# Fourteen row tiles a layer instead of seven, gathered by SyncE, with the adjacency counts and degree sums moved forward

## The chip, the cores and the metric

The kernel runs on one core of a Trainium2 chip. The metric is the device time of one execution in microseconds (us), as the median of several runs. The profile is one more execution, recorded by the hardware; its span runs from the first instruction to the last. Engines are named TensorE (PE), VectorE (DVE), ScalarE (ACT), GpSimd (POOL) and SyncE (SP).

## The reference

A graph of 2500 nodes with 256 features and 82,500 edges, sorted by destination. Two stages, each with a residual and a layer norm:

```python
# stage 1: two layers of RelGraphConv (8 relations)
for l in range(2):
    W = einsum('rb,bio->rio', coeff[l], basis[l])
    msg = einsum('ni,rio->rno', h, W)[etype, src] * norm
    h = segment_sum(msg, dst) + bias[l]          # relu after the first
x = layernorm(x + h)
# stage 2: three layers of mean aggregation
h = x @ W_in + b_in
for l in range(3):
    agg = segment_sum(h[src], dst) / max(deg, 1)
    h = relu(agg @ W_agg[l] + h @ W_self[l] + b_hid[l])
out = layernorm(x + h @ W_out + b_out)
```

## The kernel before

The edges are cut into T = 645 tiles of 128. In stage 1 each tile's 128 source rows of 256 floats are brought into SBUF and multiplied by a selection matrix that VectorE makes from destination, edge type and weight. TensorE does this for three tiles at a time (`pe_sums_of`, L1037); it adds weight times source row into (destination, relation) columns. Every 30 tiles form a window of 128 destinations, which is multiplied by the relation matrices (`pe_apply`, L885), gets its bias and is stored: in layer 0 as rows of H1 in DRAM, the table that layer 1 gathers from, in layer 1 as X1.

**Who fetches the rows.** GpSimd issues one indirect DMA for each tile (`rows_of`, L352) into 16 slots; a slot is free again when the tile that used it is summed (semaphore `s_sum`). Seven tiles of a layer, `ROW_TILES` (96, 180, ..., 600), are left out of GpSimd's list (`POOLED`). SyncE brings those as 128 plain DMAs of one row each (`sp_rows`, L1136), into one of two row buffers in the spare columns of `ei`. It reads the row addresses from SBUF into registers, eight at a time (L1133, one TENSOR_LOAD). The order is written out: `row_plan` spreads a row tile's 128 rows over the steps from the last row tile less 12 to its own less 12 (`ROW_LEAD`), and step t of SyncE's list holds what TensorE's step t stands beside.

**What else stands in SyncE's list,** in program order with the rows: in layer 0 the store of each finished window to H1 (`sp_store`, L1095, its base row loaded at L421), for which it waits on ScalarE's L784; in layer 1 the store of X1 and a load of x for two windows later (`sp_post`, L1095 and L1103), for which it waits on VectorE's L602; a load of 128 rows of the adjacency (`sp_load_rows`, L1173) for each window; and 20 loads for the degree sums (`sp_load_degrees`, L1182).

**Work beside the sums.** The dense adjacency for stage 2 is counted on TensorE from one-hot matrices (`pe_counts`, L867 and L868), ScalarE casts the counts and stores them. `adjacency_plan` says beside which tile: one count tile every 1.5 tiles from tile 90 on, and what is left up to 375 between the layers. In layer 1 from step 92 on the first mean aggregation is done in pieces (`pe_unit`), the degree sums at steps 426 to 545 (`D_BLOCK`, `pe_degree`, L1002; its data is loaded by SyncE at steps 418 + 6q), the degrees' columns at 548, the products of the nodes' own features at `OWN_TILES` (L950). Behind layer 1 follow the rest of the mean layers with TensorE busy throughout.

Of the kernel before, what the change touches and what calls it, by code (L numbers as in the profile page):

```python
# [15 lines left out]
N = 2500  # L16
D = 256
# [16 lines left out]
NG = 16  # L34
ROW_TILES = [96 + 84 * j for j in range(7)]
ROW_LEAD = 12
ROW_PARTS = range((len(ROW_TILES) + 3) // 4)
NSL = 8
# [37 lines left out]
def adjacency_plan():  # L76

    plan, a = {}, 0
    for n in range(2 * T):
        while a < T and n >= 90 + a * 1.5:  # L80
            plan.setdefault(n, []).append(a)
            a += 1
        if n == T - 1:
            while a < 375:
                plan.setdefault("between", []).append(a)
                a += 1
    assert a == T
    return plan
# [6 lines left out]

def row_plan():

    plan = {}
    for j, tile in enumerate(ROW_TILES):
        lo, hi = (ROW_TILES[j - 1] - ROW_LEAD if j else 2), tile - ROW_LEAD  # L100
        for r in range(128):
            plan.setdefault(lo + r * (hi - lo) // 128, []).append((j, r))
    return plan
# [5 lines left out]
LASTG = len(GROUPS) - 1  # L109
ROWS = row_plan()  # L110

POOLED = [n for n in range(2 * T) if n % T not in ROW_TILES]
PLACE = {n: p for p, n in enumerate(POOLED)}
# [55 lines left out]
def program(nc, x, ramp, ramp_col, src_rows, srcT, dstT, etT, wT, large, small, basis, coeff, bias, W_in, b_in, W_agg, W_self,  # L169
# [11 lines left out]
    with ExitStack() as ctx:  # L181
# [106 lines left out]
        s_land = [sem(f"s_land{i}") for i in range(NG)]  # L288
        s_ix, s_at, s_row = sem("s_ix"), sem("s_at"), [sem("s_row0"), sem("s_row1")]
        s_sel, s_sum = sem("s_sel"), sem("s_sum")  # L290
# [255 lines left out]
        def dve_unit(e, gi, c, mo):  # L546

            q, o = unit_of(gi, c, mo), sagg[:, mo, c * CH:(c + 1) * CH]
            e.wait_ge(s_part, q + 1)
            if gi == 0:  # L550
                e.tensor_copy(o, unit_bank(q)[:, 0:CH]).then_inc(s_acc, 1)
            else:
                e.wait_ge(s_acc, q - 2 * NC + 1)
                if gi > 7 and c < 3:
                    e.wait_ge(s_owns, 2 * c + mo + 1)
                e.tensor_tensor(o, unit_bank(q)[:, 0:CH], o, ALU.add).then_inc(s_acc, 1)  # L556
# [86 lines left out]
        def dve_layer(e, l):  # L643
            for t in range(T + (TAIL if l == 0 else 2)):
                n = l * T + t
                for u in range((0 if l == 0 else AHEAD) if t == 0 else t + AHEAD - 1, min(T, t + AHEAD)):
                    dve_select(e, l * T + u)
                if l == 0 and t == 20:
                    e.wait_ge(s_ix, 16 * len(ROW_PARTS))
                    at = di[0:32 * len(ROW_PARTS) - 31, 0:512]  # L650
                    e.tensor_scalar(at, at, 4 * D, None, ALU.mult).then_inc(s_at, 1)
                if l == 0 and t == 600:
# [21 lines left out]
                if l == 1:  # L674
                    for gi, c, mo in UNITS.get(t - 1, []):
                        dve_unit(e, gi, c, mo)
                    if t == 420:
# [3 lines left out]
                    if t == 549:  # L681
# [136 lines left out]
        def act_layer(e, l):  # L818
            for t in range(T + (TAIL if l == 0 else 2)):
                n = l * T + t  # L820
                if l == 0 and t == T + 10:
                    act_fix(e, 0)
                if l == 1 and t == 0:
                    act_fix(e, 1)
                if l == 1 and t % TA == TA - 1 and t < FIX - 2 * TA:
                    act_fix(e, t // TA + 2)
                if t == 0:
                    if l == 0:
                        e.wait_ge(s_zero, 1)
                    for k in range(4):  # L830
                        act_clear(e, l, 0, k)
                if t % TW in (24, 25, 26, 27) and t // TW + 1 < NW and t < T:
                    act_clear(e, l, t // TW + 1, t % TW - 24)
                for g, k in STEPS[l].get(t, []):
                    act_post(e, l, g, k)
                if l == 0 and LAG <= t < 8 * WPE + LAG:
                    act_weight(e, t - LAG)
                if t < T:
                    for a in COUNTS.get(n, []):
                        act_counts(e, a)  # L840
                if l == 1:
# [161 lines left out]

        def row_number(l, t):

            return l * len(ROW_TILES) + ROW_TILES.index(t)

        def pe_sums_of(e, l, t):
# [13 lines left out]
            for c in range(2):  # L1022
# [3 lines left out]
                for i in range(TA):  # L1026
                    n, k = l * T + t - TA + 1 + i, edge_rows(t - TA + 1 + i)
                    if n in PLACE:
                        rows = G[0:k, PLACE[n] % NG, c * 128:(c + 1) * 128]
                        if c == 0:  # L1030
                            e.wait_ge(s_land[PLACE[n] % NG], 16 * (PLACE[n] // NG + 1))
                    else:
                        q = row_number(l, n - l * T)
                        rows = GS[:, q % 2, c * 128:(c + 1) * 128]
                        if c == 0:
                            e.wait_ge(s_row[q % 2], 16 * 128 * (q // 2 + 1))
                    mm = e.matmul(bank[2 + wg % 3][:, c * 128:(c + 1) * 128], rows,  # L1037
                                  S[0:k, n % NSS, :], start=(i == 0 and not ahead), stop=(i == TA - 1))
# [17 lines left out]
        def pe_layer(e, l):  # L1056
            for t in range(T + (TAIL if l == 0 else 2)):
# [18 lines left out]
                if l == 1:  # L1076
# [7 lines left out]
                    for b in D_BLOCK.get(t, []):  # L1084
                        pe_degree(e, b)
                    if t == 548:
                        pe_columns(e)
# [24 lines left out]
        def sp_indices(e):  # L1112

            for i in ROW_PARTS:
                e.dma_start(di[32 * i:32 * i + 1, 0:512], src_rows[i:i + 1, :]).then_inc(s_ix, 16)

        def bytes_of(table):
            return table.bitcast(U8).rearrange("(o n) f -> o (n f)", o=1)

        def sp_rows(e, l, t):  # L1120

            table = bytes_of(x if l == 0 else H1)
            for j, r in ROWS.get(t, []):
                q = l * len(ROW_TILES) + j
                if l == 0 and j + r == 0:
# [3 lines left out]
                if r == 0 and q > 1:  # L1129
                    e.wait_ge(s_sum, (q - 2) // len(ROW_TILES) * T + ROW_TILES[(q - 2) % len(ROW_TILES)] + 1)  # L1130
# [7 lines left out]
        regs = []  # L1138
# [686 lines left out]
        def _(e):  # L1825
            pe_setup(e)
            with e.If(fits(e)):
                pe_layer(e, 0)
                for a in COUNTS["between"]:
                    pe_counts(e, a)  # L1830
                pe_layer(e, 1)
# [5 lines left out]
        def _(e):  # L1837
            act_setup(e)
            with e.If(fits(e)):
                act_layer(e, 0)  # L1840
                for a in COUNTS["between"]:
                    act_counts(e, a)
                act_layer(e, 1)
# [5 lines left out]
        def _(e):  # L1849
            dve_setup(e)  # L1850
            with e.If(fits(e)):
                dve_bases(e)
                dve_layer(e, 0)
                for a in COUNTS["between"]:
                    dve_counts(e, a)
                dve_layer(e, 1)
# [71 lines left out]
```

## Time and profile before

| | us |
|---|---|
| median of 3 runs | 1932.81 (1932.6 to 1933.46) |
| span of the profiled execution | 1935.5 |
| TensorE busy | 1657.1 (86%) |
| GpSimd busy | 1243.6 (64%) |
| VectorE busy | 1168.4 (60%) |
| ScalarE busy | 487.5 (25%) |
| last gather issued | 1613.93 |

The profiled execution spans 2.7 us more than the median of the runs. Layer 0 of stage 1 runs to 813 us, layer 1 to 1624 us, the mean layers to the end. Busy times are of the engines proper: SyncE, which only loads registers, waits and issues DMAs, has no row of its own there. What it does is read from the source lines and from the timeline. TensorE's granted clock is 0.963 of full over the span.

### The profile page before, as it was taken

How to read it: one execution, taken by the hardware profiler on the slowest of the kernel's cores; microseconds unless marked ns; L12 is line 12 of the kernel's file. 1: busy time of each engine (PE TensorE's matmuls, PEld its weight loads, DVE VectorE, ACT ScalarE, POOL GpSimd, SP SyncE). 2: the span in 40 equal slices, each digit the busy share in tenths (PEclk: the TensorE clock that was granted, in tenths of full speed). 3: DMA queues.
4: the chain of work that ended last, by engine and by line, in shares of the span. 5: the costliest groups of instructions: out<-in, count | busy, mean ns of one | idle time of the engine just before them, and what ended most of it. 6: DMA issues, size and time to landing. Idle time of an engine off the chain costs nothing.

```text
span 1935.5 us, 36034 instructions
## 1 busy us (share of the span) xinstructions
PE 1657.1 (86%) x9643; PEld 1378.2 (71%) x9643; DVE 1168.4 (60%) x4021; ACT 487.5 (25%) x1018; POOL 1243.6 (64%) x1311
## 2 busy tenths in 40 slices
PE   5787787887777778888899898888989999999997
PEld 3676666676566667676777787777777887777775
DVE  7978856656565656566777676775555563322344
ACT  2002111111211111122322222232455113433322
POOL 6777777777777777777777777777777773000011
PEclk9889999889999999999999999999999899999999
DMA  7344444444444444444444444445555442310011
GB/s 266 107 112 119 116 117 116 121 116 117 119 118 115 121 116 116 113 137 124 132 125 133 131 127 127 131 132 140 163 167 152 118 136 60 85 44 1 12 42 44
DMA packets 147633, 222.02 MB, mean 115 GB/s; under 512 B 81009, under 2 KB 103298, under 8 KB 147428
## 3 DMA queue, kind: packets, MB, share of 16 engines
q0 software_dynamic: 61344, 167.21, 30.4%
q1 hardware_dynamic: 49988, 38.78, 7.0%
q10 hardware_dynamic: 36096, 13.70, 2.6%
q8 instruction: 80, 1.31, 0.3%
q14 instruction: 125, 1.02, 0.2%
HBM read 202.31 MB, written 17.27 MB: 113 GB/s over the span
## 4 chain that ended last, share of the span: by engine, by line
PE 53%; DMA 31%; POOL 7%; issue 4%; DVE 3%; ACT 1%; DVEq 0%; ACTq 0%; POOLq 0%
PE bank L1037 21%; DMA RY<-in_x,si 19%; DMA RY<-H,si 12%; PE bank L1281 9%; PE bank L885 9%; POOL RY L352 7%; PE bank L935 3%; PE bank L1247 2%; PE bank L1291 2%; PE bank L868 1%; PE bank L1353 1%; PE bank L1002 1%; PE bank L852 1%; PE bank L950 1%; PE bank L908 1%
## 5 line engine op out<-in xcount | busy, mean ns | idle before, releaser
L1037 PE MATMUL bank<-RY 128*128 128x128 f32 x5104 | 768.9, 291 | 221.3 <-DMA RY<-in_x,si 146.8
L1037 PEld LDWEIGHTS bank<-RY 128*128 128x128 f32 x5104 | 678.9, 199 | 324.4 <-DMA RY<-in_x,si 187.7
L352 POOL DMA_INDIRECT RY<-in_x,si x638 | 611.2, 958 | 198.1 <-issue 136.9
L352 POOL DMA_INDIRECT RY<-H,si x623 | 595.0, 955 | 190.1 <-issue 138.4
L631 DVE TENSOR_SCALAR RY<-iot,c,wgt 128x128 f32<-128x128 f32 x1290 | 455.7, 358 | 389.3 <-PE bank L1037 388.2
L720 ACT CAST RY<-bank 128x320 uint8<-128x320 f32 x215 | 91.6, 426 | 684.2 <-PE bank L868 672.9
L509 DVE TENSOR_SCALAR RY<-iotN,bcol 128x320 bf16<-128x320 f16 x645 | 209.1, 324 | 0.0
L1281 PE MATMUL bank<-Ar,hs 125*128 125x500 f32 x800 | 203.9, 405 | 0.0
L623 DVE TENSOR_TENSOR RY<-RY,bank 128x256 f32 x430 | 178.4, 415 | 24.5 <-issue 13.0
L885 PE MATMUL bank<-RX,RY 128*128 128x256 f32 x704 | 189.1, 397 | 3.0 <-issue 1.8
L1342 POOL TENSOR_TENSOR x1b<-x1b,bo 125x256 f32<-125x256 f32 x20 | 14.8, 741 | 272.7 <-DMA x1b<-X 272.7
L885 PE MATMUL bank<-RY 128*128 128x256 f32 x704 | 184.3, 388 | 3.6 <-DVE RY L623 3.6
L868 PE MATMUL bank<-RY 128*128 128x320 bf16 x645 | 175.3, 310 | 0.5 <-DVE RY L509 0.5
L508 DVE TENSOR_SCALAR RY<-iotN,c 128x128 bf16<-128x128 f16 x645 | 175.2, 272 | 0.0
L1281 PEld LDWEIGHTS bank<-Ar,hs 125*128 125x128 f32 x800 | 150.6, 188 | 33.2 <-issue 4.6
L885 PEld LDWEIGHTS bank<-RY 128*128 128x128 f32 x704 | 129.5, 195 | 22.9 <-DVE RY L623 5.9
L885 PEld LDWEIGHTS bank<-RX,RY 128*128 128x128 f32 x704 | 130.8, 201 | 18.7 <-issue 2.0
L708 ACT COPY RY<-zero 128x576 f32<-128x576 f32 x176 | 109.5, 667 | 27.4 <-ACT RY L720 23.1
L935 PE MATMUL bank<-ArP,hsP 128*128 128x500 f32 x380 | 115.8, 425 | 0.4 <-DVE sagg L556 0.4
L777 ACT COPY RY<-bank 128x256 f32<-128x256 f32 x44 | 16.4, 373 | 314.6 <-PE bank L890 271.8
L556 DVE TENSOR_TENSOR sagg<-bank,sagg 128x500 f32<-128x500 f32 x90 | 60.6, 673 | 51.2 <-PE bank L935 51.1
L868 PEld LDWEIGHTS bank<-RY 128*128 128x128 bf16 x645 | 65.6, 102 | 27.1 <-issue 3.6
(148 smaller groups left out, 1311.3 us busy)
## 6 DMA issues: line engine op xcount, KB each, us to landing
ei<-in_x SPq DMA_DIRECT2D x896, 1.0 KB
ei<-H SPq DMA_DIRECT2D x896, 1.0 KB
RY<-in_x,si POOLq DMA_INDIRECT x638
RY<-H,si POOLq DMA_INDIRECT x623
Ad<-RY ACTq DMA_DIRECT2D x215, 40.0 KB
A<-Ad SPq DMA_DIRECT2D x22, 312.5 KB, 3.3
D<-Ad SPq DMA_DIRECT2D x20, 305.2 KB
RX<-in_basis ACTq DMA_DIRECT2D x2, 2048.0 KB, 21.7
```

Of the source, the lines that this page charges most:

```text
L352: e.indirect_dma_start(G[0:k, slot, :], None, table, bass.IndirectOffsetOnAxis(ap=index[0:k, t:t + 1], axis=0)).then_inc(s_land[slot], 16)
L508: e.tensor_scalar(Mr[:, u % NSL, :], iotN[:, 0:128], c1[:, u:u + 1], None, ALU.is_equal)
L509: e.tensor_scalar(Nr[:, u % NSL, :], iotN[:, :], bcol[:, u:u + 1], None, ALU.is_equal).then_inc(s_hot, 1)
L623: e.tensor_tensor(o, o, bank[2 + wg % 3][:, 0:256].rearrange("p (q c) -> p q c", c=16), ALU.add).then_inc(s_za, 1)
L631: e.tensor_scalar(S[:, v % NSS, :], iot[:, :], c2[:, u:u + 1], wgt[:, u:u + 1], ALU.is_equal, ALU.mult).then_inc(s_sel, 1)
L708: e.copy(o, zero[:, 0:1].to_broadcast([128, 4 * ZC])).then_inc(s_clear, 1)
L720: e.copy(Aw8[:, w % 4, :], bank[6 + w % 2][:, 0:NB]).then_inc(s_aw8, 1)
L868: e.matmul(b[:, 0:NB], Mr[0:k, a % NSL, :], Nr[0:k, a % NSL, :], start=(a == 0), stop=(i == TA - 1)).then_inc(s_cnt, 1)
L885: mm = e.matmul(bank[0][:, 0:256], ZA[:, s, q, 0:128], W[:, c, r * 256:(r + 1) * 256], start=(q == 0), stop=(g == 0 and q == 15))
L935: mm = e.matmul(unit_bank(q)[:, 0:CH], hsP[:, g % NP, part, mo * 128:(mo + 1) * 128], ArP[:, n % NV, :], start=(i + part == 0), stop=(i == ...
L1037: mm = e.matmul(bank[2 + wg % 3][:, c * 128:(c + 1) * 128], rows, S[0:k, n % NSS, :], start=(i == 0 and not ahead), stop=(i == TA - 1))
L1281: mm = e.matmul(bank[bs[mo]][:, 0:CH], hs[0:PB, j, q, mo * 128:(mo + 1) * 128], Ar[0:PB, n % NR, :], start=(j == 0 and q == 0), stop=(j == ...
```

## The change

SyncE gets 14 row tiles a layer, at 50 + 43j (50, 93, ..., 609); the seven of before were 84 apart. It loads 16 addresses at once instead of 8. The addresses now lie in 14 partitions of `ei`, one row tile in each, and no longer in 2 partitions of `di`; their DMA is issued ahead of that of the zero rows, and VectorE scales them at step 8 instead of 20. A second set of row tiles for ScalarE is written into the program, but its two lists are empty.

The counts come one every 1.25 tiles and the block between the layers is gone, so that they end at step 250 of layer 1 instead of 411. The degree loads start at step 262, 7 apart (before 418, 6 apart), the degree sums at 270, the columns at 416, and six of the eight own products before step 623 lie at 420 to 494 instead of 551 to 571.

```diff
-ROW_TILES = [96 + 84 * j for j in range(7)]
+SP_TILES = [50 + 43 * j for j in range(14)]
+ACT_SPANS = ([], [])
 ROW_LEAD = 12
+ROW_AT = 16
...
-        while a < T and n >= 90 + a * 1.5:
+        while a < T and n >= 90 + a * 1.25:
...
-        if n == T - 1:
-            while a < 375:
-                plan.setdefault("between", []).append(a)
-                a += 1
...
-D_LOAD = {418 + 6 * q: q for q in range(JB)}
+D_LOAD = {262 + 7 * q: q for q in range(JB)}
...
-    D_BLOCK.setdefault(426 + 6 * b_ // 5, []).append(b_)
-D_SUM = {451 + 24 * c: c for c in range(NC)}
+    D_BLOCK.setdefault(270 + 7 * b_ // 5, []).append(b_)
+D_SUM = {300 + 28 * c: c for c in range(NC)}
...
-OWN_TILES = (551, 555, 559, 563, 567, 571, 623, 628)
+OWN_TILES = (420, 424, 428, 432, 490, 494, 623, 628)
...
-                if l == 0 and t == 20:
-                    e.wait_ge(s_ix, 16 * len(ROW_PARTS))
-                    at = di[0:32 * len(ROW_PARTS) - 31, 0:512]
-                    e.tensor_scalar(at, at, 4 * D, None, ALU.mult).then_inc(s_at, 1)
+                if l == 0 and t == 8:
+                    e.wait_ge(s_ix, 16)
+                    e.tensor_scalar(row_at, row_at, 4 * D, None, ALU.mult).then_inc(s_at, 1)
...
-                if r % 8 == 0:
-                    half, at = divmod(j * 128 + r, 512)
-                    _, regs[:] = nc.values_load_multi_w_load_instructions(
-                        di[32 * half:32 * half + 1, at:at + 8], engines=[mybir.EngineType.SP], min_val=0, max_val=(N - 1) * 4 * D,
-                        skip_runtime_bounds_check_because="indices are numbers of rows of the table")
-                e.dma_start(GS8[r:r + 1, q % 2, :], table[0:1, bass.ds(regs[r % 8], 4 * D)]).then_inc(s_row[q % 2], 16)
+                if r % ROW_AT == 0:
+                    sp_at[:] = row_addresses(j, r, mybir.EngineType.SP)
+                e.dma_start(GS8[r:r + 1, q % 2, :], table[0:1, bass.ds(sp_at[r % ROW_AT], 4 * D)]).then_inc(s_row[q % 2], 16)
...
         def sp_layer(e, l):
             if l == 0:
+                sp_indices(e)
                 sp_zero_rows(e)
-                sp_indices(e)
```

SyncE's list in layer 0 from one store of a finished window to the next, which are 30 tiles apart; `ei<-in_x` is a row of a row tile, `bai` the window's base row. Before:

```order
L1095 DMA H<-RY 128x256
L1136 DMA ei<-in_x 1x1024
L1133 TENSOR_LOAD di
L1136 DMA ei<-in_x 1x1024 x8
L1133 TENSOR_LOAD di
L1136 DMA ei<-in_x 1x1024 x8
L1133 TENSOR_LOAD di
L1136 DMA ei<-in_x 1x1024 x8
L1133 TENSOR_LOAD di
L1136 DMA ei<-in_x 1x1024 x8
L1133 TENSOR_LOAD di
L1136 DMA ei<-in_x 1x1024 x8
```

The same place after the change:

```order
L1101 DMA H<-RY 128x256
L1147 DMA ei<-in_x 1x1024
L1127 TENSOR_LOAD ei
L1147 DMA ei<-in_x 1x1024 x16
L1127 TENSOR_LOAD ei
L1147 DMA ei<-in_x 1x1024 x16
L1127 TENSOR_LOAD ei
L1147 DMA ei<-in_x 1x1024 x16
L1127 TENSOR_LOAD ei
L1147 DMA ei<-in_x 1x1024 x16
L1127 TENSOR_LOAD ei
L1147 DMA ei<-in_x 1x1024 x16
```

Between two stores SyncE issued 45 or 46 rows with six loads; now it issues 89 or 90 with five or six loads of twice the length.

SyncE's list in layer 1 where the degree loads (`D<-Ad`) stand among the rows (`ei<-H`). Before:

```order
L1182 DMA D<-Ad 125x5x500
L1136 DMA ei<-H 1x1024
L1133 TENSOR_LOAD di
L1136 DMA ei<-H 1x1024 x8
L1182 DMA D<-Ad 125x5x500
L1133 TENSOR_LOAD di
L1136 DMA ei<-H 1x1024 x8
L1133 TENSOR_LOAD di
L1136 DMA ei<-H 1x1024
L1182 DMA D<-Ad 125x5x500
```

After the change:

```order
L1206 DMA D<-Ad 125x5x500
L1147 DMA ei<-H 1x1024 x13
L1127 TENSOR_LOAD ei
L1147 DMA ei<-H 1x1024 x8
L1206 DMA D<-Ad 125x5x500
L1147 DMA ei<-H 1x1024 x8
L1127 TENSOR_LOAD ei
L1147 DMA ei<-H 1x1024 x13
L1206 DMA D<-Ad 125x5x500
```

Before there were 9 rows between two degree loads, six steps apart; now there are 21, seven steps apart. All 20 degree loads still stand between rows.

## Rows read from the trace of the kernel before

**Rows 1.** The page's groups: count | busy us, mean ns | idle before

```profile
L352 POOL DMA_INDIRECT RY<-in_x,si x638 | 611.2, 958 | 198.1 <-issue 136.9
```

**Rows 2.** Line L352, two stretches: ns min/median/max, first and last start

```profile
L352 POOL DMA_INDIRECT RY<-in_x,si x637: 942/947/1682, 4.4 to 807.3; - x160
...
L352 POOL DMA_INDIRECT RY<-H,si x612: 942/947/1219, 839.2 to 1608.9; - x153
```

**Rows 3.** Waits of GpSimd: for whom, us in total, times, longest

```profile
POOL RY L352 <- issue: 279.3, 916, 0.3
...
POOL RY L352 <- PE bank L1037: 109.2, 358, 0.4
```

**Rows 4.** Two windows: PE, PEld, DVE, ACT, POOL busy us, clock, DMA share, GB/s

```profile
700.00:800.00 100.00, 79.44 (x483) 66.51 (x482) 60.79 (x244) 16.76 (x35) 75.63 (x81) 0.93 0.42 117
1500.00:1600.00 100.00, 98.55 (x583) 84.52 (x582) 61.71 (x163) 20.27 (x44) 75.52 (x80) 0.95 0.45 127
```

**Rows 5.** Waits of SyncE's queue

```profile
SPq L421 <- ACT RY L784: 358.1, 22, 38.7
SPq L421 <- DVE RY L602: 247.3, 22, 24.1
```

**Rows 6.** Lines L1133 and L1136: whole, layer 0, parts of layer 1, singles

```profile
L1133 SPq TENSOR_LOAD <-di x224: 526/786/977, 47.1 to 1545.8; - x112
...
L1136 SPq DMA_DIRECT2D ei<-in_x x896: 224/228/289, 47.9 to 729.2; - x180
...
L1136 SPq DMA_DIRECT2D ei<-H x635: 224/228/329, 828.9 to 1336.9; - x159
...
L1136 SPq DMA_DIRECT2D ei<-H x180: 227/228/2261, 1336.9 to 1479.1; - x180
...
L1133 SPq TENSOR_LOAD <-di x1: 712/712/712, 47.1 to 47.1; - x1
...
L1133 SPq TENSOR_LOAD <-di x1: 535/535/535, 828.3 to 828.3; - x1
```

**Rows 7.** Timeline of SyncE's DMAs, start of layer 1: start us, us, line, count

```profile
828.91 12.71 SPq L1136 DMA_DIRECT2D ei<-H  x30
...
882.65 0.38 SPq L1095 DMA_DIRECT2D X<-RY  x1
...
884.27 17.88 SPq L1136 DMA_DIRECT2D ei<-H  x42
...
903.63 1.28 SPq L1136 DMA_DIRECT2D ei<-H  x4
```

**Rows 8.** Line L421, loads of one value: after rows, after idling, a pair

```profile
L421 SPq TENSOR_LOAD <-bai x1: 537/537/537, 841.7 to 841.7; - x1
...
L421 SPq TENSOR_LOAD <-bai x1: 443/443/443, 112.4 to 112.4; - x1
...
L421 SPq TENSOR_LOAD <-bai x2: 280/392/503, 881.7 to 883.1; - x2
```

**Rows 9.** Timeline of SyncE's DMAs: a row just behind a degree load

```profile
1370.01 1.53 SPq L1136 DMA_DIRECT2D ei<-H  x1
```

**Rows 10.** Timeline of SyncE at the start

```profile
38.58 0.54 SPq L1115 DMA_DIRECT2D di<-in_src_rows  x2
```

**Rows 11.** TensorE on the row buffer: tile 600 of layer 0, of layer 1

```profile
L1037 PE MATMUL bank<-RY,ei x4: 273/275/275, 759.6 to 760.4; 128*128 128x128 f32 x4
...
L1037 PE MATMUL bank<-RY,ei x4: 270/274/275, 1573.5 to 1574.3; 128*128 128x128 f32 x4
```

**Rows 12.** Timeline: the last sums of layer 0, last gather and sums of layer 1

```profile
812.19 1.16 PE L1037 MATMUL bank<-RY 68*128 68x128 f32 x8 [1.47 <-DMA RY<-in_x,si]
...
1613.93 1.10 POOL L352 DMA_INDIRECT RY<-H,si  x1 [0.30 <-PE bank L1037]
...
1622.90 1.50 PE L1037 MATMUL bank<-RY 128*128 128x128 f32 x12
```

**Rows 13.** Line L868, the count matmuls of TensorE

```profile
L868 PE MATMUL bank<-RY x645: 296/299/474, 123.7 to 1329.1; 128*128 128x320 bf16 x161, 68*128 68x320 bf16 x1
```

More of the change, by code:

```diff
@@ L34 @@
 NG = 16
-ROW_TILES = [96 + 84 * j for j in range(7)]
+SP_TILES = [50 + 43 * j for j in range(14)]
+ACT_SPANS = ([], [])
+ACT_TILES = [tile for spans in ACT_SPANS for _, tile in spans]
+ACT_FIRST = (0, len(ACT_SPANS[0]))
+BY_ROWS = {l * T + tile for l in range(2) for tile in SP_TILES + [tile for _, tile in ACT_SPANS[l]]}
 ROW_LEAD = 12
-ROW_PARTS = range((len(ROW_TILES) + 3) // 4)
+ROW_AT = 16
 NSL = 8
@@ L93, in chores_by, with row_plan @@
     return min(NCH, sum(1 + (u % 3 == 0) if u < 40 else 1 - u % 2 for u in range(t + 1 - LAG)))
-def row_plan():
+def row_plan(spans):
     plan = {}
-    for j, tile in enumerate(ROW_TILES):
-        lo, hi = (ROW_TILES[j - 1] - ROW_LEAD if j else 2), tile - ROW_LEAD
+    for j, (begin, tile) in enumerate(spans):
         for r in range(128):
-            plan.setdefault(lo + r * (hi - lo) // 128, []).append((j, r))
+            plan.setdefault(begin + r * (tile - ROW_LEAD - begin) // 128, []).append((j, r))
     return plan
@@ L109 @@
 LASTG = len(GROUPS) - 1
-ROWS = row_plan()
-POOLED = [n for n in range(2 * T) if n % T not in ROW_TILES]
+SP_ROWS = row_plan([(SP_TILES[j - 1] - ROW_LEAD if j else 2, tile) for j, tile in enumerate(SP_TILES)])
+ACT_ROWS = [row_plan(spans) for spans in ACT_SPANS]
+POOLED = [n for n in range(2 * T) if n not in BY_ROWS]
 PLACE = {n: p for p, n in enumerate(POOLED)}
@@ L156 @@
 BLOCKS = {block_of(gi, c, i): (gi, c, i) for gi in range(LASTG + 1) for c in range(NC) for i in range(len(GROUPS[gi]))}
+UNIT_TILE = {unit_of(gi_, c_, mo_): t_ for t_, us in UNITS.items() for gi_, c_, mo_ in us}
 BLOCKS_AT = {}
@@ L244, in program @@
         GS8 = ei[:, 0:512].bitcast(U8).rearrange("p (s f) -> p s f", f=4 * D)
+        GA = di[:, 0:512].bitcast(F32).rearrange("p (s f) -> p s f", f=256)
+        GA8 = di[:, 0:512].bitcast(U8).rearrange("p (s f) -> p s f", f=4 * D)
+        row_at = ei[0:len(SP_TILES) + len(ACT_TILES), 512:640]
         mask = sb("mask", [128, NW], F32)
@@ L288, in program @@
         s_land = [sem(f"s_land{i}") for i in range(NG)]
-        s_ix, s_at, s_row = sem("s_ix"), sem("s_at"), [sem("s_row0"), sem("s_row1")]
+        s_ix, s_at = sem("s_ix"), sem("s_at")
+        s_row, s_rowA = [sem("s_row0"), sem("s_row1")], [sem("s_rowA0"), sem("s_rowA1")]
         s_sel, s_sum = sem("s_sel"), sem("s_sum")
@@ L553, in dve_unit @@
                 e.wait_ge(s_acc, q - 2 * NC + 1)
-                if gi > 7 and c < 3:
+                if c < 4 and UNIT_TILE[q] > OWN_TILES[2 * c + mo]:
                     e.wait_ge(s_owns, 2 * c + mo + 1)
@@ L833, in act_layer @@
                     act_clear(e, l, t // TW + 1, t % TW - 24)
+                act_rows(e, l, t)
                 for g, k in STEPS[l].get(t, []):
@@ L1031, in pe_sums_of @@
                             e.wait_ge(s_land[PLACE[n] % NG], 16 * (PLACE[n] // NG + 1))
-                    else:
-                        q = row_number(l, n - l * T)
+                    elif n - l * T in SP_TILES:
+                        q = l * len(SP_TILES) + SP_TILES.index(n - l * T)
                         rows = GS[:, q % 2, c * 128:(c + 1) * 128]
@@ L1036, in pe_sums_of @@
                             e.wait_ge(s_row[q % 2], 16 * 128 * (q // 2 + 1))
+                    else:
+                        q = ACT_TILES.index(n - l * T, ACT_FIRST[l])
+                        rows = GA[:, q % 2, c * 128:(c + 1) * 128]
+                        if c == 0:
+                            e.wait_ge(s_rowA[q % 2], 16 * 128 * (q // 2 + 1))
                     mm = e.matmul(bank[2 + wg % 3][:, c * 128:(c + 1) * 128], rows,
@@ L1085, in pe_layer @@
                         pe_degree(e, b)
-                    if t == 548:
+                    if t == 416:
                         pe_columns(e)
@@ L1112, in sp_indices, with row_addresses @@
         def sp_indices(e):
-            for i in ROW_PARTS:
-                e.dma_start(di[32 * i:32 * i + 1, 0:512], src_rows[i:i + 1, :]).then_inc(s_ix, 16)
+            e.dma_start(row_at, src_rows).then_inc(s_ix, 16)
         def bytes_of(table):
             return table.bitcast(U8).rearrange("(o n) f -> o (n f)", o=1)
+        def row_addresses(row, r, engine):
+            _, values = nc.values_load_multi_w_load_instructions(
+                ei[row:row + 1, 512 + r:512 + r + ROW_AT], engines=[engine], min_val=0, max_val=(N - 1) * 4 * D,
+                skip_runtime_bounds_check_because="indices are numbers of rows of the table")
+            return values
+        sp_at, act_at = [], []
         def sp_rows(e, l, t):
-            table = bytes_of(x if l == 0 else H1)
-            for j, r in ROWS.get(t, []):
-                q = l * len(ROW_TILES) + j
+            table, many = bytes_of(x if l == 0 else H1), len(SP_TILES)
+            for j, r in SP_ROWS.get(t, []):
+                q = l * many + j
                 if l == 0 and j + r == 0:
@@ L1129, in sp_rows, with act_rows @@
                 if r == 0 and q > 1:
-                    e.wait_ge(s_sum, (q - 2) // len(ROW_TILES) * T + ROW_TILES[(q - 2) % len(ROW_TILES)] + 1)
-                if r % 8 == 0:
-                    half, at = divmod(j * 128 + r, 512)
-                    _, regs[:] = nc.values_load_multi_w_load_instructions(
-                        di[32 * half:32 * half + 1, at:at + 8], engines=[mybir.EngineType.SP], min_val=0, max_val=(N - 1) * 4 * D,
-                        skip_runtime_bounds_check_because="indices are numbers of rows of the table")
-                e.dma_start(GS8[r:r + 1, q % 2, :], table[0:1, bass.ds(regs[r % 8], 4 * D)]).then_inc(s_row[q % 2], 16)
-        regs = []
+                    e.wait_ge(s_sum, (q - 2) // many * T + SP_TILES[(q - 2) % many] + 1)
+                if r % ROW_AT == 0:
+                    sp_at[:] = row_addresses(j, r, mybir.EngineType.SP)
+                e.dma_start(GS8[r:r + 1, q % 2, :], table[0:1, bass.ds(sp_at[r % ROW_AT], 4 * D)]).then_inc(s_row[q % 2], 16)
+        def act_rows(e, l, t):
+            table = bytes_of(x if l == 0 else H1)
+            for j, r in ACT_ROWS[l].get(t, []):
+                q = ACT_FIRST[l] + j
+                if q + r == 0:
+                    e.wait_ge(s_at, 1)
+                if l == 1 and j + r == 0:
+                    e.wait_ge(s_h1, 16 * NW)
+                if r == 0 and q > 1:
+                    e.wait_ge(s_sum, (T if q - 2 >= ACT_FIRST[1] else 0) + ACT_TILES[q - 2] + 1)
+                if r % ROW_AT == 0:
+                    act_at[:] = row_addresses(len(SP_TILES) + q, r, mybir.EngineType.Activation)
+                e.dma_start(GA8[r:r + 1, q % 2, :], table[0:1, bass.ds(act_at[r % ROW_AT], 4 * D)]).then_inc(s_rowA[q % 2], 16)
         def sp_layer(e, l):
             if l == 0:
+                sp_indices(e)
                 sp_zero_rows(e)
-                sp_indices(e)
             for t in range(T + (TAIL if l == 0 else 2)):
@@ L1828, in _ @@
                 pe_layer(e, 0)
-                for a in COUNTS["between"]:
-                    pe_counts(e, a)
                 pe_layer(e, 1)
@@ L1840, in _ @@
                 act_layer(e, 0)
-                for a in COUNTS["between"]:
-                    act_counts(e, a)
                 act_layer(e, 1)
@@ L1853, in _ @@
                 dve_layer(e, 0)
-                for a in COUNTS["between"]:
-                    dve_counts(e, a)
                 dve_layer(e, 1)
@@ L1899 @@
         "ramp_col": np.arange(128, dtype=np.float32).reshape(128, 1),
-        "src_rows": np.ascontiguousarray(np.concatenate([np.asarray(src).reshape(-1)[128 * t:128 * (t + 1)] for t in
-                                                         ROW_TILES + [0] * (4 * len(ROW_PARTS) - len(ROW_TILES))]).reshape(-1, 512)),
+        "src_rows": np.ascontiguousarray(np.stack([np.asarray(src).reshape(-1)[128 * t:128 * (t + 1)] for t in SP_TILES + ACT_TILES])),
         "srcT": tiles(src, 0),
```

6 lines of the change are left out of this document (2 added, 4 removed).

## The prediction

> **What bounds the kernel now.** I read the page's groups first. GpSimd issues one gather for nearly every tile of 128 edges, 638 in each layer, each about 0.95 us long [rows 1]. Then line L352 by stretch: 637 gathers between 4.4 and 807.3 us, 612 between 839.2 and 1608.9 us [rows 2]. That is 802.9/636 = 1.262 us and 769.7/611 = 1.260 us a gather, without a break from the start to 1614 us. The waits of GpSimd say why: 279.3 us of its idle time are "issue", 0.3 us behind each gather, and only 109.2 us name TensorE [rows 3]. The windows show room beside it: TensorE is busy 79.4 of 100 us in layer 0, and 98.6 only in the stretch from 1500 us [rows 4]. So up to 1614 us the end moves by 1.26 us for each gather that GpSimd does or doesn't issue; behind it stands a fixed tail.
>
> The second thing to read is SyncE, which counts nowhere as busy. It feeds the seven row tiles of each layer by 128 DMAs of one row each. Its waits show 358.1 + 247.3 us in which it stood before its stores, for ScalarE's L784 and VectorE's L602 [rows 5]. These are its whole reserve over two layers. The question of this case is whether the doubled row work fits into it.
>
> **What the change removes.** Seven gathers a layer: 14 x 1.26 = 17.6 us, if nothing else becomes late.
>
> **What it adds: SyncE's work.** I price it in three pieces.
>
> A row: the DMA's issue takes 228 ns at the median [rows 6], with a move and gaps between. Undisturbed bursts give the pitch: 30 rows in 12.71 us with three loads inside, 42 rows in 17.88 us with five [rows 7]. With 0.82 us for a load (786 ns and gaps) that is 10.2/30 = 0.341 and 13.8/42 = 0.328 us. I take 0.334.
>
> An address load: before it brings 8 values, after it 16, half as many. No row shows 16. Eight values cost 786 ns at the median, one value after a burst of rows 537, so seven more cost 249 ns; two other pairs in equal surroundings, 712 against 443 and 535 against 280, give 269 and 255 [rows 6, 8]. That is about 36 ns a value, so 16 values are 786 + 285 = 1.07 us, 1.10 with the gap. Bounds: 0.81 if the number did not matter, 1.40 if the second eight cost twice as much a value. I take 1.10, since three pairs agree. A row tile is then 128 x 0.334 + 8 x 1.10 = 51.6 us of SyncE (before: 42.8 + 16 x 0.82 = 55.9).
>
> Its other work: in layer 1 the pair "store X, load x" 2.6 us (its first base load at 881.7 [rows 8], rows go on at 884.27), a load of Ad rows 1.48 us (902.15 to 903.63) [rows 7], a load for the degrees, without a base load, some 0.38 us; in layer 0 a store of H with its base load, half of the pair, 1.3 us. And the row behind such a degree load is slow: 1.53 us where 0.23 is normal [rows 6, 9]. The whole layer's rows up to 1337 us have a maximum of 329 ns, those from there to 1482 us, where the 20 degree loads are, one of 2261 [rows 6]. I charge 1.3 us more for each.
>
> **The budget.** Row tiles now come every 43 tiles, of which 42 are gathered: 42 x 1.26 = 52.9 us. SyncE needs 51.6 us for the rows of one, plus in layer 0 1.4 stores, 1.8 us: 53.4. In layer 1 it needs 51.6 + (19 x 2.6 + 20 x 1.48 + 20 x 1.68)/14 = 51.6 + 8.0 = 59.6 us. It loses 0.5 us a period in layer 0 and 6.7 us in layer 1. Its idle time can't be used, since it becomes late rather than waiting.
>
> *Layer 0.* SyncE can begin its rows at about 39 us: the zero rows that it waits for are in at 38.5 us, and the indices, awaited now by VectorE eight tiles in, are issued ahead of them [rows 10]. Rows of tile 609 are issued at 39 + 14 x 51.6 + 19 x 1.3 = 786 us and landed at 789. Before, tile 600 is multiplied at 760 us, so tile 609 near 771 [rows 11]. From there 35 tiles remain. GpSimd is 16 ahead, but TensorE must do them all: 0.99 us a tile (79.4 us of 80 gathers' time [rows 4]) and 0.04 for the denser counts, 36 us. The layer's sums end at 825 where they ended at 813.3 [rows 12]: 12 us later.
>
> *Layer 1.* Its rows wait for the last store of H, as before at 828.1 us, so now at 840. SyncE's sum up to tile 609 is 14 x 59.6 = 834 us: landed at 840 + 834 + 3 = 1677. Before, tile 600 is at 1574.3, tile 609 near 1588 [rows 11]: 89 us later. TensorE's 35 tiles after it took 36 us before, to 1624.4 [rows 12], and take the same, less 5 us by the points below. Sum: +84 us.
>
> **The other parts.** Counts without the break: 74 or so more of them in layer 0, at 0.30 us of TensorE [rows 13] and a share of the carry products, some 30 us in a layer where it idles over 150 us; the five of the break, about 2 us, leave the chain between the layers. Degree sums and own products leave the stretch where TensorE is 98.6% busy (100 matmuls and six products) [rows 4]. What TensorE is behind there is small: last gather issued at 1613.9, landed some 3.9 us later, last sum done at 1624.4 [rows 12], so at most 6.6 us of lag could be won. I count 3 for it and 2 for the break. VectorE's earlier wait for the indices can hold it 3 to 6 us near 32 us (the nearest landings are 2.9 us and 6.4 us); six selections are made ahead, and tile 50 waits longer for its rows (landed at 39 + 51.6 + 3 = 94 us, due at about 80). Of the degree loads TensorE needs each eight tiles behind the place where SyncE issues it. With SyncE twelve tiles behind, TensorE will be held there too, but by the same queue, so it adds nothing to the sum.
>
> **A rule that speaks against it.** The Trainium skill, "Runtime: NRT & Kernel Launch", section "Instruction fetch mechanics", gives register loads about 200 ns a register. By it 16 values would be 0.79 + 8 x 0.2 = 2.4 us, as an estimate from that page 145 us more a layer than my sum and a time near 2307 us. The pairs in [rows 6, 8] show 36 ns a value from this memory, and I hold to them.
>
> **The sum.** The profiled execution spans 1935.5 us, its time in the runs is 1932.8 at the median, 2.7 less. 1935.5 + 84 - 2.7 = 2017 us.
>
> **Rivals.**
> 1. *The load costs 0.81 us whatever it brings.* SyncE saves 8 x 0.29 = 2.3 us a tile, 32.5 a layer. Layer 0 would have rows at 757 us, ahead of the gathers (771 - 8.8 = 762), and end 9 us earlier, at 804.5. Layer 1: 819 + 834 - 32.5 + 3 = 1623.5, 35.5 later than before, less 5: 1932.8 + 30.5 = 1963 us. For it: a load's length varies from 526 to 977 ns with its surroundings, more than by its values. Against it: the three pairs. 18%.
> 2. *SyncE keeps up* (the other side). With each row at 0.32 us, under any pitch of [rows 7], each load 0.55 us and no slow row behind the degree loads, layer 1 needs 14 x 45.4 + 49 + 30 + 8 = 723 us and is done at 819 + 723 + 3 = 1545, which is before the gathers: 17.6 us are won, and up to 5 of lag: 1910 to 1915 us. It decides below 52.9 us a period in both layers; in layer 1 that needs 0.28 us a row with all else as I price it. Nothing in the medians says so. 5%; between it and no change another 3%.
> 3. *SyncE slows down further* when A loads and degree loads meet twice as many rows in its queue, or the load of 16 costs 1.40 us: 8 x 0.3 x 14 = 34 us a layer, 68 in all: 2085 us. For it: the slow rows of 2.26 us. 12%.
> My own forecast, SyncE the bound in both layers at about these prices, has 62%.
>
> **How the numbers follow.** About 0.2% is what a measurement of this kernel can tell from no change. My case's own range is 1985 to 2055 (a row pitch wrong by 0.008 us moves 14 us a layer, a load wrong by 0.1 us 11 us a layer). To hold 8 in 10 it must take in rival 1: 1945 to 2065. Faster 0.05, same 0.03, slower 0.92.
>
> **What would show it.** Right: SyncE's waits for L784 and L602 nearly vanish up to its last row; GpSimd's gathers come at about 53.4 us for 42 in layer 0 and near 60 us for 42 in layer 1 (70 in 100 us instead of 80), its idle time naming TensorE; TensorE waits long before the matmuls that read the row buffer, at most 14 times a layer; the address load has a median near 1.07 us; the last row of layer 0 is issued near 786 us, that of layer 1 near 1674. Wrong at the load's price: a median near 0.8. Wrong altogether: waits of SyncE before its stores remain at ten and more us each through layer 1, and 80 gathers in 100 us.

## The result, and the profile after

| | before | after |
|---|---|---|
| median of the runs, us | 1932.75 | 2063.38 (2062.62 to 2065.39) |
| ratio, 95% interval | | 1.0675 [1.0662, 1.0689] |
| span of the profiled execution | 1935.5 | 2061.2 |
| mean granted TensorE clock | 0.963 | 0.901 |

The change costs 130.6 us. The prediction said slower, by SyncE's list, and gave 84. The lines below answer to those of before; line numbers are those of the kernel that each line comes from.

Gathers: two lines of the page's groups (to compare with [rows 1]) and line L357 by stretch ([rows 2]; duration ns min/median/max, first and last start):

```profile
L357 POOL DMA_INDIRECT RY<-H,si x616 | 585.8, 951 | 285.9 <-PE bank L1043 144.1
L357 POOL DMA_INDIRECT RY<-in_x,si x631 | 605.5, 960 | 229.7 <-issue 144.3
...
L357 POOL DMA_INDIRECT RY<-in_x,si x630: 940/946/1602, 4.3 to 833.2; - x158
...
L357 POOL DMA_INDIRECT RY<-H,si x599: 940/946/1199, 879.8 to 1728.8; - x200
```

A gather itself is as long as before. But 630 of them now need 828.9 us and 599 need 849.0: 1.318 and 1.420 us a gather, where it was 1.262 and 1.260. The waits of GpSimd ([rows 3]) and of SyncE's queue ([rows 5]) say on whom:

```profile
POOL RY L357 <- issue: 289.6, 947, 0.9
...
POOL RY L357 <- PE bank L1043: 236.6, 314, 11.2
```

```profile
SPq L426 <- ACT RY L788: 48.3, 3, 20.0
SPq L426 <- DVE RY L607: 46.6, 3, 22.4
```

GpSimd's wait for TensorE to free a slot has doubled, with single waits up to 11.2 us. SyncE's 605 us of reserve have shrunk to 95, in three waits of each kind where there were 22, and in both layers all three begin behind the layer's last row. The prediction called this disappearance the first sign of its case. The chain of work that ended last, followed back from the end, says the same (section 4 of the page; shares of the span):

```profile
SPq 63%; PE 18%; issue 14%; DMA 2%; DVE 1%; ACT 1%; ACTq 0%; DVEq 0%; POOL 0%; POOLq 0%
```

The windows of layer 0 and of the stretch of the degree loads in layer 1 (as [rows 4]):

```profile
700.00:800.00 100.00, 76.51 (x524) 66.59 (x522) 67.63 (x285) 19.71 (x42) 73.27 (x78) 0.89 0.42 116
...
1300.00:1400.00 100.00, 78.25 (x444) 63.62 (x442) 39.32 (x113) 38.43 (x78) 58.92 (x63) 0.90 0.45 126
```

78 gathers in 100 us in layer 0 and 63 in the stretch of the degree loads, where there were 81 and 80 in [rows 4]. Over layer 1 the 1.420 us are 70 in 100 us, as forecast.

SyncE's two lines (as [rows 6]):

```profile
L1127 SPq TENSOR_LOAD <-ei x224: 984/1247/1470, 38.7 to 1697.1; - x112
...
L1147 SPq DMA_DIRECT2D ei<-in_x x1792: 224/228/314, 40.0 to 806.2; - x200
...
L1147 SPq DMA_DIRECT2D ei<-H x1792: 227/228/1615, 861.6 to 1705.9; - x200
```

Rows cost what they did. A load of 16 addresses takes 1.247 us; 1.07 was predicted. The last row of layer 0 is issued at 806.2 us (predicted 786), that of layer 1 at 1705.9 (1674).

TensorE at the last row tile of each layer and at the end of layer 1 (timeline: start us, us, what; in brackets the idle time before; as [rows 11, 12]):

```profile
807.69 0.76 PE L1043 MATMUL bank<-RY,ei 128*128 128x128 f32 x2 [14.03 <-DMA ei<-in_x]
...
1707.63 0.77 PE L1043 MATMUL bank<-RY,ei 128*128 128x128 f32 x2 [10.55 <-DMA ei<-H]
...
1735.00 1.10 POOL L357 DMA_INDIRECT RY<-H,si  x1 [0.30 <-issue]
...
1749.67 1.50 PE L1043 MATMUL bank<-RY 128*128 128x128 f32 x12
```

It idles 14.0 and 10.6 us and starts 1.5 and 1.7 us behind the issue of the last row. To compare with before, one must know when tile 609 was multiplied there. The prediction estimated it from tile 600, near 771 and 1588 us. In the timeline of the kernel before the group of three tiles that begins with 609 starts at 768.4 us in layer 0, and in layer 1 here:

```profile
1583.45 1.50 PE L1037 MATMUL bank<-RY 128*128 128x128 f32 x12
```

Where the 125.7 us between the two profiles arise:

| place | before | after | later by |
|---|---|---|---|
| tile 609 of layer 0 multiplied | 768.4 | 807.7 | 39 |
| layer 0's last sum done | 813.3 | 847.3 | 34 |
| first row of layer 1 issued | 828.9 | 861.6 | 33 |
| tile 609 of layer 1 | 1583.5 | 1707.6 | 124 |
| layer 1's last sum done | 1624.4 | 1751.2 | 127 |
| end | 1935.5 | 2061.2 | 126 |

### The profile page after: what moved, and what is told of

It reads as the page before. It is cut to its first block, busy times and chain, and to the rows that moved or that the text cites. A ratio compares the mean times of both kernels' runs of the same rounds, so it can differ in the third digit from the quotient of the medians.

```text
span 2061.2 us, 39603 instructions
## 1 busy us (share of the span) xinstructions
PE 1630.0 (79%) x9643; PEld 1383.5 (67%) x9643; DVE 1159.3 (56%) x4021; ACT 486.1 (24%) x1018; POOL 1229.3 (60%) x1297
## 3 DMA queue, kind: packets, MB, share of 16 engines
q14 instruction: 153, 1.25, 0.2%
## 4 chain that ended last, share of the span: by engine, by line
SPq 63%; PE 18%; issue 14%; DMA 2%; DVE 1%; ACT 1%; ACTq 0%; DVEq 0%; POOL 0%; POOLq 0%
SPq L1147 45%; SPq L1127 13%; PE bank L1305 9%; SPq L426 2%; PE bank L890 2%; PE bank L1271 2%; PE bank L1043 2%; PE bank L1315 2%; DMA D<-Ad 1%; SPq L1101 1%; DMA RX<-in_basis 1%; PE bank L1377 1%; SPq L1197 0%; SPq L1109 0%; PE bank L994 0%
## 5 line engine op out<-in xcount | busy, mean ns | idle before, releaser
L357 POOL DMA_INDIRECT RY<-H,si x616 | 585.8, 951 | 285.9 <-PE bank L1043 144.1
L357 POOL DMA_INDIRECT RY<-in_x,si x631 | 605.5, 960 | 229.7 <-issue 144.3
L1043 PE MATMUL bank<-RY 128*128 128x128 f32 x5048 | 700.3, 289 | 44.2 <-issue 16.3
L1043 PEld LDWEIGHTS bank<-RY 128*128 128x128 f32 x5048 | 666.1, 204 | 82.3 <-issue 24.9
L636 DVE TENSOR_SCALAR RY<-iot,c,wgt 128x128 f32<-128x128 f32 x1290 | 449.9, 360 | 470.9 <-PE bank L1043 468.4
L1043 PE MATMUL bank<-RY,ei 128*128 128x128 f32 x112 | 36.5, 426 | 257.0 <-DMA ei<-in_x 174.9
L1043 PEld LDWEIGHTS bank<-RY,ei 128*128 128x128 f32 x112 | 27.3, 299 | 262.7 <-DMA ei<-in_x 112.2
L514 DVE TENSOR_SCALAR RY<-iotN,bcol 128x320 bf16<-128x320 f16 x645 | 201.1, 312 | 0.0
L873 PE MATMUL bank<-RY 128*128 128x320 bf16 x645 | 178.4, 310 | 10.6 <-DVE RY L514 9.4
L890 PEld LDWEIGHTS bank<-RY 128*128 128x128 f32 x704 | 132.0, 198 | 26.0 <-DVE RY L628 7.3
L940 PE MATMUL bank<-ArP,hsP 128*128 128x500 f32 x380 | 120.1, 438 | 0.4 <-DVE sagg L561 0.4
```

The costliest lines, as they stand in the source:

```text
L357: e.indirect_dma_start(G[0:k, slot, :], None, table, bass.IndirectOffsetOnAxis(ap=index[0:k, t:t + 1], axis=0)).then_inc(s_land[slot], 16)
L514: e.tensor_scalar(Nr[:, u % NSL, :], iotN[:, :], bcol[:, u:u + 1], None, ALU.is_equal).then_inc(s_hot, 1)
L636: e.tensor_scalar(S[:, v % NSS, :], iot[:, :], c2[:, u:u + 1], wgt[:, u:u + 1], ALU.is_equal, ALU.mult).then_inc(s_sel, 1)
L873: e.matmul(b[:, 0:NB], Mr[0:k, a % NSL, :], Nr[0:k, a % NSL, :], start=(a == 0), stop=(i == TA - 1)).then_inc(s_cnt, 1)
L890: mm = e.matmul(bank[0][:, 0:256], ZA[:, s, q, 0:128], W[:, c, r * 256:(r + 1) * 256], start=(q == 0), stop=(g == 0 and q == 15))
L940: mm = e.matmul(unit_bank(q)[:, 0:CH], hsP[:, g % NP, part, mo * 128:(mo + 1) * 128], ArP[:, n % NV, :], start=(i + part == 0), stop=(i == ...
```

## The experiments

**Without SyncE's row work.** Only 8 of the 128 rows of each row tile are fetched, so the sums of these tiles are incomplete.

```diff
             for j, r in SP_ROWS.get(t, []):
+                if r >= 8:
+                    continue
...
-                            e.wait_ge(s_row[q % 2], 16 * 128 * (q // 2 + 1))
+                            e.wait_ge(s_row[q % 2], 16 * 8 * (q // 2 + 1))
```

> This kernel is the changed one, but SyncE fetches only the first 8 of the 128 rows of each row tile (and TensorE waits for 8), so SyncE has next to no row work; the sums of the row tiles are left incomplete. Theory (gathers set the time up to the end of stage 1, 1.26 us each, SyncE's row work is all that the change lost): 1932.8 - 14 x 1.26 = 1915 us, up to 5 us less for the lag of TensorE that the moved degree work takes away: 1909 to 1916 us. Rival (the earlier counts, degree sums and own products cost time themselves): 1925 us or more.

Measured 1919.16 us (ratio 0.992 [0.9903, 0.9937]), 144 us under the changed kernel with all its other parts in place. SyncE's waits are back:

```profile
SPq L426 <- ACT RY L788: 697.9, 22, 43.7
SPq L426 <- DVE RY L607: 480.2, 22, 45.0
```

So the whole loss, and more, is SyncE's row work. The gain over the kernel before is 13.6 us, not 17.6 or more, so the time lies between my theory's range (to 1916) and the rival's (from 1925); the third run says why.

**Row tiles alone.** The degree and count work of the kernel before, beside 14 row tiles. The lines left out put the counts between the layers, the degree sums and the columns back as well.

```diff
-        while a < T and n >= 90 + a * 1.25:
+        while a < T and n >= 90 + a * 1.5:
...
-D_LOAD = {262 + 7 * q: q for q in range(JB)}
+D_LOAD = {418 + 6 * q: q for q in range(JB)}
...
-OWN_TILES = (420, 424, 428, 432, 490, 494, 623, 628)
+OWN_TILES = (551, 555, 559, 563, 567, 571, 623, 628)
```

> Fourteen row tiles a layer as in the changed kernel, but counts, degree loads, degree sums and own products where they were before. Theory (SyncE's list sets the time, and its sum is the same wherever the degree loads stand in it): 2063 us, within 8. Rival (a third or more of the loss comes from the moved work: degree loads and sums that TensorE waits for when SyncE is late): 2020 us or less.

Measured 2063.48 us, the changed kernel's 2063.38 again. The last row of layer 1 is issued at 1706.4 us against 1705.9. A list that is the bound takes its sum, wherever an item stands in it. The rival (2020 us or less) is out.

**The plan alone.** Seven row tiles, 84 apart, with the rest of the change.

```diff
-SP_TILES = [50 + 43 * j for j in range(14)]
+SP_TILES = [96 + 84 * j for j in range(7)]
```

> Seven row tiles 84 apart as before, but 16 addresses at a load, and counts, degree sums and own products as in the changed kernel. Theory: gathers are the bound and SyncE has room, so only the break between the layers (2 us) and TensorE's lag (up to 3) can go: 1927 to 1933 us. Rival (the moved work costs time): 1940 us or more.

Measured 1936.40 us, ratio 1.0013 [1.0003, 1.0023]: neither. It costs 0.6 to 4.4 us where I expected a gain of up to 5. With it the first run reads well: 14 gathers fewer on top of this plan are 1936.4 - 1919.2 = 17.2 us, 1.23 us each. What in the plan costs is not settled: in its profile the last sum is done 6.7 us behind the issue of the last gather (10.5 before), but layer 0's last sum comes some 2 us later.

**Eight addresses a load.** `ROW_AT = 8` in the changed kernel.

> The changed kernel with 8 addresses a load instead of 16 (16 loads a row tile). Theory (a load's time goes by the number of its values: 8 take 0.79 us as before the change, 16 take 1.25): 16 x 0.82 - 8 x 1.28 = 2.9 us more a row tile, 28 of them: 2063 + 80 = 2143 us. Rival (the load is longer because of where the addresses now lie, 1.25 us for 8 too): 16 x 1.28 - 8 x 1.28 = 10.2 us a tile, about 2350 us.

Measured 2154.2 us, 91 more. The load:

```profile
L1127 SPq TENSOR_LOAD <-ei x448: 527/791/959, 38.8 to 1793.1; - x150
```

From the same place in memory eight values take what they took before the change, so the 1.247 us are the price of 16 values. In layer 0 the rows run from 39.6 to 852.3 us, 46.5 us longer than in the changed kernel, 3.3 us for each of 14 tiles (2.9 expected); in layer 1 they take 888.1 us, 43.8 longer. Together that is the 91 us. This edit changes the loads in SyncE's list and not the rows that are fetched, so it is the list, and not the rows' traffic, that sets the time.

**Four runs on another chip.** The next four ran where the kernel before itself takes 2274.07 us.

> The changed kernel with the 20 degree loads issued by ScalarE at the same steps instead of by SyncE. Theory (SyncE's list is the bound in layer 1 and each degree load costs it 0.38 us and 1.3 us of a slow row behind it): 20 x 1.68 = 34 us less, 2030 us. Rival (the slow rows come from the DMA engines being busy with the degree data, whoever issues it): only the issue goes, 2063 - 8 = 2055 us.

> The changed kernel with 32 addresses a load (4 loads a row tile). Measured: 1 value 0.54 us, 8 values 0.79, 16 values 1.25, so 57 ns a value for the second eight. If it goes on so, 32 values take 2.16 us: 4 x 2.19 - 8 x 1.28 = -1.5 us a row tile, 2063 - 41 = 2022 us. Rival (the time is the same 1.25 us for more values): 4 x 1.28 - 8 x 1.28 = -5.1 us a tile, about 1920 us or where the gathers bound it.

> Eleven row tiles a layer, 55 apart (50 to 600), 16 addresses a load, counts and degree work where they were before the change. Theory (a period has 54 gathers, 68.0 us, and SyncE needs 52.8 us for a row tile and 2.4 us of stores in layer 0, 52.8 + 7.5 us in layer 1, some 73 in the stretch of the degree loads, where 12 tiles of lead cover it): SyncE keeps up and eight gathers are saved, 1932.8 - 8 x 1.26 = 1923 us. Rival (SyncE becomes the bound again where the degree loads stand): 1935 us or more.

> Twelve row tiles a layer, 50 apart (50 to 600), degree loads issued by ScalarE, the rest as in the run with eleven. Theory (49 gathers are 61.7 us, SyncE needs 52.8 + 6.8 = 59.6 us in layer 1): ten gathers are saved, 1932.8 - 12.6 = 1920 us. Rival (it starts layer 1 late and has no reserve): SyncE is late by up to 15 us and the time is 1930 us or more.

Their ratios to before were 1.1767, 1.1656, 1.0592 and 1.0963. Below stand line L1127 of the run with 32 addresses, and line L1151 (a row's issue) of the run with eleven tiles from 100 to 700 us:

```profile
L1127 SPq TENSOR_LOAD <-ei x112: 8/2104/2291, 38.9 to 2271.3; - x112
```

```profile
L1151 SPq MOVE ei<-in_x x880: 2/29/768, 100.5 to 699.2; - x176
L1151 SPq DMA_DIRECT2D ei<-in_x x880: 2/227/777, 100.6 to 699.3; - x176
```

Medians are as on the first chip, but a register move that takes 29 ns takes up to 768: time and again the sequencer stands still for some 0.7 us. In layer 0 of the run with the degree loads on ScalarE a row tile starts every 79 us, where it is 55 in the changed kernel with the same row plan, so a kernel that leans on SyncE loses more here. These times say nothing on the theories. What stays is the load of 32 values, 2.10 us at the median (2.16 expected): 54 ns a value more. At 4 x 2.13 us a row tile against 8 x 1.28 that would be 1.7 us less; its effect on the time was not measured on a usual chip. The other three were run again, on a third chip where before takes 1933.39 us.

**Degree loads on ScalarE.**

```diff
-                    if t in D_LOAD:
-                        sp_load_degrees(e, D_LOAD[t])
...
 def act_layer ...
                 if l == 1:
+                    if t in D_LOAD:
+                        sp_load_degrees(e, D_LOAD[t])
```

> The changed kernel with the 20 degree loads issued by ScalarE instead of SyncE, once more, on a chip where the kernel before takes its usual time. Theory (each degree load costs SyncE 0.38 us and 1.3 us of a slow row behind it, and SyncE is the bound): 2063 - 34 = 2030 us. Rival (the slow rows come from busy DMA engines, whoever issues the load): 2055 us.

Measured 2038.67 us (ratio 1.0546 [1.052, 1.0572]), 24.7 us less than the changed kernel. Its rows of layer 1:

```profile
L1149 SPq DMA_DIRECT2D ei<-H x1792: 227/228/486, 862.9 to 1682.1; - x200
```

The slow rows are gone (longest 486 ns, in the changed kernel 1615), and the rows of layer 1 take 819.2 us instead of 844.3: 25.1 us for 20 loads, 1.25 each, which is all that the time shows. The mechanism stands, and the rival (2055 us, slow rows whoever issues the load) is out. My 1.68 us were too much, which is why the time is 9 us above the 2030 expected.

**Eleven row tiles.** `SP_TILES = [50 + 55 * j for j in range(11)]`, count and degree work as before.

> Eleven row tiles a layer, 55 apart, degree and count work as before the change, once more. Theory: SyncE keeps up (72 us of work against 68 only in the stretch of the degree loads, inside the lead of 12 tiles), eight gathers are saved: 1923 us. Rival (SyncE is late there): 1935 us or more.

Measured 1939.93 us, ratio 1.0033 [1.0022, 1.0044]. The theory fails, though SyncE waits again for 176 and 108 us. Two places show. The first row tile at 50 is too early: layer 0's rows begin at 41.4 us, so the tile is multiplied at 93.7 and GpSimd idles 4.7 us there. And in the degree stretch SyncE is late for the degree loads, which lead their use by eight tiles only. ScalarE's waits for them are, in this order, those of the kernel before, the changed one, this one, and the run before this one, in which ScalarE issues the degree loads:

```profile
ACT RY L765 <- DMA D<-Ad: 20.7, 8, 3.4
```

```profile
ACT RY L769 <- DMA D<-Ad: 115.8, 20, 10.8
```

```profile
ACT RY L773 <- DMA D<-Ad: 60.2, 16, 7.3
```

```profile
ACT RY L769 <- DMA D<-Ad: 35.9, 11, 5.6
```

TensorE waits behind ScalarE, and GpSimd, with its slots full, idles 7.6 us from 1512 us on. The rival (SyncE is late there, 1935 us or more) has it. I had kept the lead of the rows in mind (12 tiles) and not that of the degree loads.

**Twelve row tiles, degree loads on ScalarE.** Both edits above, `SP_TILES = [50 + 50 * j for j in range(12)]`.

> Twelve row tiles a layer, 50 apart, degree loads issued by ScalarE, once more. Theory: 59.6 us of SyncE's work against 61.7 us of gathers in layer 1, ten gathers are saved: 1920 us. Rival (no reserve is left for the late start of layer 1): 1930 us or more.

Measured 1927.58 us, ratio 0.9972 [0.9962, 0.9982]: 5.8 us faster than before and the only version here with all its work in place that is measurably faster than it. That is less than half of the 12.6 us expected, between the theory (1920) and the rival (1930 or more). SyncE waits 123.1 and 73.7 us, so it does have a reserve; the degree wait is 26.0 us. Of what is missing some 5 us go at the first row tile:

```profile
94.20 0.94 POOL L361 DMA_INDIRECT RY<-in_x,si  x1 [5.34 <-PE bank L1049]
```

**Ten row tiles.** `[60 + 60 * j for j in range(10)]`, degree loads on SyncE.

> Ten row tiles a layer, 60 apart (60 to 600), the rest as with eleven. Theory: SyncE has room everywhere (52.8 + 8.2 us, 14 more for degree loads, against 74.3 us of gathers), six gathers are saved: 1932.8 - 7.6 = 1925 us. Rival (each row tile costs time of its own, whatever room SyncE has): 1932 us or more.

Measured 1933.25 us, ratio 1.0007 [0.9995, 1.002]. No gain, where 7.6 us were expected. The first row tile at 60 holds nobody up for long, but the degree wait is 49.2 us, and GpSimd waits for TensorE after it:

```profile
1514.12 0.94 POOL L361 DMA_INDIRECT RY<-H,si  x1 [1.99 <-PE bank L1047]
...
1518.90 0.94 POOL L361 DMA_INDIRECT RY<-H,si  x1 [1.35 <-PE bank L1047]
```

In the profiles the last gather is issued at 1610.1 us, 3.8 us earlier than before: about half of what six gathers are worth. These gaps explain part of the other half; the rest is open. The rival's figure (each row tile costs time of its own, 1932 us or more) was met, so this run doesn't rule it out. The run with twelve tiles speaks against it as the whole story, since it gained with more row tiles than this one.

## Why the prediction was right, and what was mis-sized

Right, point by point. *Gathers set the pace:* 14 fewer gave 17.2 us on the same plan. *SyncE becomes late and sets the end in both layers:* its waits vanish, and taking its work away gives back 144 us. *Its idle time can't be used:* 95 us of waits are left, all behind the last rows of the layers. *The placing of the other work is not in the sum:* 2063.48 against 2063.38. *Being held for degree data adds nothing to the sum while SyncE is the bound:* ScalarE waits 115.8 us for it, and yet the list's length alone accounts for the time.

The number was less good than that. 2063.38 lies outside the range that I gave my own case (1985 to 2055), and within the wider one (1945 to 2065) by under 2 us, which is luck. It is also nearer to rival 3's 2085 (22 us) than to my 2017 (46 us). Of that rival's two causes one is half there: the load costs 1.28 us with its gap, between my 1.10 and its 1.40. The other, slower rows behind the large loads, is not: they cost less than I charged.

The terms, measured:

| term of the sum | predicted | measured | effect on the end |
|---|---|---|---|
| load of 16 addresses with its gap, 224 of them | 1.10 us | 1.28 us | +40 |
| degree load and the slow row behind it, 20 | 1.68 us | 1.25 us | -9 |
| landing of the last row, two layers | 3 us | 1.5 us | -3 |
| layer 0's last 35 tiles | 36 us | 39.6 us | +4 |
| layer 1's last 35 tiles | 36 us | 43.5 us | +8 |
| credit for lag and break | -5 us | none seen | +5 |
| time against the profile's span | -2.7 us | +2 us | +5 |

Together they give 50 us, where 2017 missed 2063 by 46. Some 2 of the difference are that layer 1's rows begin 14.3 us behind layer 0's last sum (15 predicted) and that the end is 310.0 us behind layer 1's last sum (311.1 before). With the first two terms put right, SyncE's list of layer 0 is 747 + 20 = 767 us (measured from 38.7 to 806.4: 767.7), that of layer 1 834 + 20 - 9 = 845 (844.3 between its first and last row).

The step that carried most of the error is "about 36 ns a value, so 16 values are 1.07 us". I drew a line through 1 and 8 values and went on past its end, with three pairs that agreed with each other but all spanned the same piece. The second eight cost 57 ns each. The bounds (0.81 to 1.40) held it.

The rule of the Trainium skill ("Runtime: NRT & Kernel Launch", "Instruction fetch mechanics", about 200 ns a register) is not borne out for these loads: they cost 57 ns a value from 8 to 16 and 54 from 16 to 32. The page speaks of registers loaded from HBM, and these values lie in SBUF; no run here loads registers from HBM.

The last stretches have two other causes. One is my place for tile 609: in layer 1 of before its group starts at 1583.5 us, so the 35 tiles took 40.9 us and not 36. That is 4.9 us of the 7.5.

The other is TensorE's clock. Behind its waits for rows it runs at the lower of its two levels: the granted clock is 0.50 of full (1.2 of 2.4 GHz) just behind both waits and 0.95 to 1.00 in the stretches after (windows as in [rows 4]):

```profile
807.00:812.00 5.00, 4.31 (x17) 3.93 (x18) 1.96 (x9) 0.00 (x0) 3.16 (x4) 0.54 0.27 79
812.00:820.00 8.00, 8.00 (x59) 7.20 (x57) 5.78 (x23) 1.22 (x3) 4.95 (x6) 1.00 0.34 94
...
1707.00:1712.00 5.00, 4.37 (x17) 4.07 (x17) 1.12 (x3) 0.00 (x0) 1.32 (x2) 0.50 0.30 84
1712.00:1720.00 8.00, 8.00 (x49) 7.25 (x48) 4.42 (x11) 0.32 (x1) 4.36 (x5) 0.95 0.60 148
```

All matmuls on the row buffers, before and after, show that it is so behind most row tiles (ns min/median/max):

```profile
L1037 PE MATMUL bank<-RY,ei x56: 270/275/422, 133.9 to 1574.3; 128*128 128x128 f32 x56
```

```profile
L1043 PE MATMUL bank<-RY,ei x112: 273/421/584, 92.7 to 1709.3; 128*128 128x128 f32 x112
```

I priced the catching up at TensorE's rate when it is never held. What the clock costs in layer 1 can be read from the next group of sums, of before and after:

```profile
1586.97 1.50 PE L1037 MATMUL bank<-RY 128*128 128x128 f32 x12
```

```profile
1713.68 1.50 PE L1043 MATMUL bank<-RY 128*128 128x128 f32 x12
```

From tile 609's group to this one 3.5 us pass before the change and 6.1 after it. This one comes 126.7 us later than before, and so, within 0.5 us, does each of the ten groups behind it. So the clock costs some 2.6 us, all of it in the first stretch behind the wait, and nothing later. In layer 0 the granted clock is 0.50 a second time, from 829 to 832 us; how the 3.6 us there divide between it and the denser counts was not worked out. The clock was not changed by itself in any run.

The 2.7 us were a mistake of mine in another way: the profiled execution of before, with its span of 1935.5 us, is longer than each of the 37 later executions of that kernel on usual chips (1927.2 to 1934.3). In the later runs the time is about 2 us above the span.

## What to carry to other kernels

Before work is moved to an engine that looks idle, add up its program-order list against the time that the work beside it takes between two deadlines, register loads and issue slots included; SyncE's 605 us of waits looked ample, and 896 more rows a layer at 0.41 us overdrew them. Ask of every item in that list what its own lead is: the rows had 12 tiles, the degree loads eight, and these ran out first. And when a price has to be read off a line, look whether the new size lies between the measured ones or beyond them.

## What the runs showed of the hardware

- SyncE's load of registers from SBUF, just behind DMA issues: 0.54 us for 1 value (a single load), and at the median 0.79 for 8, 1.25 for 16, 2.10 for 32 (the last on the slow chip, where SyncE's median for a register move was 29 ns and for a row's issue 228 as elsewhere).
- A row DMA of 1 KB costs SyncE 0.32 us of its list at the median, and the same with twice the number of rows. Behind a DMA of 305 KB from its own queue rows stall: 0.93 us more a load in the changed kernel than in the run where ScalarE issues these loads, and single rows take up to 2.26 us in the kernel before. With ScalarE issuing, no row takes more than 0.49 us, 0.26 above the usual.
- One chip ran the kernel before 18% slower. In the four kernels profiled there SyncE's sequencer stood still for about 0.7 us at a time, in one of nine register moves with eleven row tiles, while a matmul took 299 ns and a gather 949 at the median (298 and 946 in the changed kernel on a usual chip).
